# Wide-head attention with three-pass products over two tiles, and its first tiles prepared inside the feed-forward layer before it

## Chip, cores and metric

One core of one Trainium2 chip. The metric is the device time of one execution in microseconds, as a median of several.

## The reference, cut to what matters

Eight layers run one after another on `x` of 32 x 64 tokens of 128 values. With `LN` the plain layer norm, the two that matter are:

```python
# layer 1: feed-forward, 128 -> 512 -> 128
x = x + gelu(LN(x) @ w1 + b1) @ w2 + b2
# layer 2: attention with 16 heads of 64 over the 64 context tokens of the same batch
xn = layernorm(LN(x), ln_gamma, ln_beta)
q = (xn @ w_q).reshape(B, SQ, 16, 64)
k, v = split(ctx @ w_kv)
attn = softmax(einsum('bqhd,bkhd->bhqk', q * 64 ** -0.5, k))
out = einsum('bhqk,bkhd->bqhd', attn, v).reshape(B, SQ, 1024) @ w_out + b_out
x = x + out * tanh(gate)
```

Ahead stands an attention with 16 heads of 8, behind a mixture of 16 experts; four more layers follow. Everything is float32.

## The kernel before

The 2048 tokens are 16 tiles of 128 rows (`NT`), two batches a tile. The residual `X` stays in SBUF. Each engine has its own instruction stream; semaphores order them, and the order within an engine is written out by hand.

`wide_head_attention` is a pipeline over tiles. In step n TensorE does in this order: scores of tile n-2, turned rows of n-1, turned probabilities of n-3, queries of n-1, turned outputs of n-4, keys of n, weighed values of n-3, projection of n-4, values of n-2. Steps 0 to 6 and the last are written out, the rest is a loop of two steps (`pipeline`, `Fori`). Queries (L976) and keys (L939) of a tile are eight float32 products each, of a 128x128 block of weights with 128 columns of tokens; the trace records each float32 product as two instructions. They go through the two PSUM banks `J0` and `J1`, which turned rows (`J0`) and values use too. ScalarE evicts them: L1075 turned rows, L1083 turned probabilities, L1091 queries, L1107 keys, L1099 turned outputs, L1112 exponentials. VectorE has the norms (L139 to L154), the maximum and subtraction (L1157, L1159), the sum, the division, the residual and the copy of the values (L1197). GpSimd computes the reciprocal roots (L150) and copies a tile of context for the values (L1124). TensorE starts the layer (`m.begin`) when the feed-forward layer's last residual addition is done.

`experts` is also the first feed-forward layer (tag `F0`). It already uses three passes instead of a float32 product: operands are split into a high part in the type `fp32r` and a low part (the value less its high part), and L1431 to L1433 add high x high, high x low and low x high in one PSUM group, 512 columns each. The second product (L1464) is float32. Beside it (`beside`) the routing of a later layer is worked out: VectorE's chain `choose` (L1818 to L1846), TensorE's rank products (L1865 to L1867), tables (L1930) fed by GpSimd's `owners` (L1922).

Of the kernel before, what the change touches and what calls it, by code (L numbers as in the profile page):

```python
# [863 lines left out]
def wide_head_attention(sh, m, tag, start, w):  # L864

# [7 lines left out]
    L = Layer()  # L873
    with ExitStack() as scope:
        def sb(name, shape, dt=F32):
            return scope.enter_context(nc.sbuf_tensor(f"{tag}_{name}", shape, dt))

        outer = Norm(sh, sb, f"{tag}_outer", m)
# [4 lines left out]
        qT = sb("qT", [P, 2, HP, P])  # L883
        ctx1 = sb("ctx1", [P, 2, P])
        kT = sb("kT", [P, 2, HP, 2, S])
        v = sb("v", [P, 2, 2, HP, dh])
        prob = sb("prob", [P, 2, H, S])
# [6 lines left out]
        tmp = sb("tmp", [P, 2, P])  # L894

# [14 lines left out]
    x1_ready, xn_ready, xnT_ready, xnT_ps = signal("x1_ready", NT), signal("xn_ready", NT), signal("xnT_ready", NT), signal("xnT_in_psum", NT)  # L910
    q_ps, q_ready = signal("q_in_psum", 2 * NT), signal("q_ready", 2 * NT)
    k_ps, k_ready = signal("k_in_psum", 2 * NT), signal("k_ready", 2 * NT)
    v_ps, v_ready, ctx1_ready = signal("v_in_psum", 2 * NT), signal("v_ready", 2 * NT), signal("ctx1_ready", NT)
# [6 lines left out]
    LO, HI, END = 7, NT - 1, NT + 5  # L920

    def begun(n):

        return isinstance(n, int) and tag in m.stats_after

    def follower():
        return m.stats_after[tag]

    def tensor(pe):
        m.begin(pe, start)  # L930
        pe.wait_ge(*m.dispatch.owner_ready(1))

        def keys(t, p):
# [9 lines left out]
        def values(t, p):  # L943
            pe.wait_ge(*ctx1_ready(t + 1))
            wv = w["v"].rearrange("p (c u d) -> p c u d", u=2, d=dh)
            for b in range(2):
                if before_end(t, 2):
                    pe.wait_ge(*k_ready(2 * t + b + 5))
                elif before_end(t, 1):
                    pe.wait_ge(*q_ready(2 * t + 3 + b))  # L950
                else:
                    pe.wait_ge(*v_ready(2 * t - 1 + b))
                for u in range(2):
                    mm = pe.matmul((J1, J0)[b][u * S:(u + 1) * S, :], ctx1[:, p, b * S:(b + 1) * S], wv[:, :, u, :],  # L954
                                   start=True, stop=True)
                mm.then_inc(v_ps.sem, 1)

        def turn_x(t, p):
            pe.wait_ge(*xn_ready(t + 1))
            if past(t, 2):  # L960
                pe.wait_ge(*v_ready(2 * t - 2))
            else:
                pe.wait_ge(*k_ready(2 * t + 2))
            pe.transpose(J0[:, 0:P], xn[:, p, :], m.ident[:, :]).then_inc(xnT_ps.sem, 1)  # L964

        def queries(t, p):
            pe.wait_ge(*xnT_ready(t + 1))
            for j in range(2):
                if j == 0:
                    if past(t, 2):  # L970
                        pe.wait_ge(*v_ready(2 * t - 3))
                    else:
                        pe.wait_ge(*k_ready(2 * t + 1))
                for c in range(4):
                    cc = 4 * j + c
                    mm = pe.matmul((J1, J0)[j][:, c * P:(c + 1) * P], w["q"][:, cc * P:(cc + 1) * P], xnT[:, p, :],  # L976
                                   start=True, stop=True)
                mm.then_inc(q_ps.sem, 1)

        def scores(t, p):  # L980
            pe.wait_ge(*q_ready(2 * t + 2))
            pe.wait_ge(*k_ready(2 * t + 2))
            if past(t, 1):
                pe.wait_ge(*sub_ready(t))
            apart(pe, m)
            for c in range(HP):
                for b in range(2):
                    for u in range(2):
                        rows, toks = slice(u * S, (u + 1) * S), slice(b * S, (b + 1) * S)
                        mm = pe.matmul(pS[toks, u, c * S:(c + 1) * S], qT[rows, p, c, toks], kT[rows, p, c, b, :],  # L990
                                       start=True, stop=True)
            mm.then_inc(scores_ready.sem, 1)

        def turn_probs(t, p):
            pe.wait_ge(*prob_ready(t + 1))
            if past(t, 2):
                pe.wait_ge(*tmp_ready(t - 1))
            elif past(t, 1):
# [7 lines left out]
        def weigh_values(t, p):  # L1006
            pe.wait_ge(*probT_ready(2 * t + 2))
            pe.wait_ge(*v_ready(2 * t + 2))
            if past(t, 1):
# [10 lines left out]
        def turn_out(t, p):  # L1020
            pe.wait_ge(*on_ready(t + 1))
            if before_end(t, 1):
# [13 lines left out]

        def step(n, p):
            q = 1 - p
            if live(n - 2):
                scores(n - 2, p)  # L1040
            if live(n - 1):
                turn_x(n - 1, q)
            if live(n - 3):
                turn_probs(n - 3, q)
            if begun(n) and n == NT + 2:
                pe.wait_ge(*v_ready(2 * NT))
                follower().turn(pe, 0)
            if live(n - 1):
                queries(n - 1, q)
            if live(n - 4):  # L1050
                turn_out(n - 4, p)
            if live(n):
                keys(n, p)
            if live(n - 3):
                weigh_values(n - 3, q)
            if begun(n) and n == NT + 3:
                follower().turn(pe, 1)
            if live(n - 4):
                project(n - 4, p)
            if live(n - 2):  # L1060
                values(n - 2, p)

        pipeline(pe, step, LO, HI, END)

    def scalar(act):
        m.begin(act, start)

        def step(n, p):
            q = 1 - p
            if live(n - 1):  # L1070
                t = n - 1
                act.wait_ge(*xnT_ps(t + 1))
                if past(t, 2):
                    act.wait_ge(*q_ps(2 * t - 2))
                act.activation(xnT[:, q, :], J0[:, 0:P], ACT.Identity, bias=w["beta"],  # L1075
                               scale=w["gamma"]).then_inc(xnT_ready.sem, 1)
            if live(n - 3):
                t = n - 3
                if past(t, 2):
# [5 lines left out]
            if live(n - 1):  # L1085
                t = n - 1
                if past(t, 2):
                    act.wait_ge(*scores_ready(t - 1))
                for j in range(2):
                    act.wait_ge(*q_ps(2 * t + j + 1))  # L1090
                    act.activation(qT[:, q, 4 * j:4 * j + 4, :].rearrange("p c q -> p (c q)"), (J1, J0)[j],  # L1091
                                   ACT.Copy).then_inc(q_ready.sem, 1)
            if live(n - 4):
                t = n - 4
# [1983 lines left out]
```

## Time and profile before

| | |
|---|---|
| median of 3 runs | 964.1 us (961.65 to 967.59) |
| span of the profiled execution | 1010.8 us, 46.7 above the median |
| TensorE busy | 783.2 us (77%), 8041 instructions |
| VectorE busy | 608.2 us (60%) |
| ScalarE busy | 486.4 us (48%) |
| GpSimd busy | 372.9 us (37%) |
| mean granted TensorE clock | 0.889 of full speed |
| chain that ended last | TensorE 67%, VectorE 9%, ScalarE 5% |

The time of the profiled execution is given as its span alone, from its first to its last instruction. All other times below are from that execution too, in us from its start. A busy share says how long an engine worked, not whether another waited for it.

### The profile page before, as it was taken

To read this page: it belongs to the slowest core of one execution; us is meant where nothing else is said; L and a number is where in the kernel's file an instruction comes from. 1 tells how busy PE (TensorE), PEld (TensorE's weight loads), DVE (VectorE), ACT (ScalarE), POOL (GpSimd) and SP (SyncE) were. 2 spreads that over 40 slices of the span, in tenths; PEclk is the share of its full clock that TensorE was granted. 3 is DMA by queue.
4 is the path that set the end of the run, shared out by engine and by line. 5 is a ranking of instruction groups with operands and counts; after the bars stand their busy time and mean duration, and the time that the engine had idled before them with its cause. 6 is when DMAs were issued, how large, how long until landed. Compare 5 with 4: busy or idle time off the path is not lost.

```text
span 1010.8 us, 24129 instructions
## 1 busy us (share of the span) xinstructions
PE 783.2 (77%) x8041; PEld 646.4 (64%) x8041; DVE 608.2 (60%) x1568; ACT 486.4 (48%) x984; POOL 372.9 (37%) x492
## 2 busy tenths in 40 slices
PE   6998899999999789996477775667677559969005
PEld 3766787888888679985476664667676526644005
DVE  3886747777777667767353224632222368867895
ACT  3886434555444344432154435334444357745753
POOL 5663421111111331111566653155556535550810
PEclk9999699999999979999699989579989769978557
DMA  6300000000000000033332213101111300000001
GB/s 187 96 0 1 1 1 3 2 3 0 0 0 3 1 11 19 21 102 103 95 100 88 64 41 105 42 19 43 40 37 45 85 23 3 0 1 1 0 0 42
DMA packets 49218, 36.06 MB, mean 36 GB/s; under 512 B 7665, under 2 KB 44978, under 8 KB 49138
## 3 DMA queue, kind: packets, MB, share of 16 engines
q1 hardware_dynamic: 43420, 24.45, 8.5%
q0 software_dynamic: 4992, 10.23, 3.6%
q8 instruction: 48, 0.79, 0.3%
q10 hardware_dynamic: 726, 0.33, 0.1%
q14 instruction: 32, 0.26, 0.1%
HBM read 26.73 MB, written 8.26 MB: 35 GB/s over the span
## 4 chain that ended last, share of the span: by engine, by line
PE 67%; DVE 9%; another core or an unknown queue 6%; issue 5%; ACT 5%; DMA 3%; DVEq 2%; POOL 2%; ACTq 1%; SPq 1%; POOLq 0%
PE psum L2118 9%; PE psum L1464 7%; PE psum L2143 4%; PE psum L1034 3%; PE psum L976 3%; PE psum L954 3%; PE psum L939 3%; PE psum L2442 2%; PE psum L1431 2%; PE psum L1432 2%; PE psum L1433 2%; PE psum L323 2%; PE psum L1016 2%; PE psum L663 2%
## 5 line engine op out<-in xcount | busy, mean ns | idle before, releaser
L2118 PE MATMUL psum<-E_XT,E_weights 128*128 128x128 f32 x780 | 114.3, 298 | 52.4 <-ACT E_XT L2198 27.7
L2118 PEld LDWEIGHTS psum<-E_XT,E_weights 128*128 128x128 f32 x780 | 103.0, 209 | 61.2 <-ACT E_XT L2198 30.8
L2266 POOL DMA_INDIRECT y_scratch<-E_y,route_place_of x78 | 78.8, 1010 | 83.2 <-DVE E_y L2321 37.8
L2258 POOL DMA_INDIRECT E_rows<-rows_scratch,route_token_of x78 | 76.4, 979 | 32.1 <-issue 25.5
L1723 DVE SCALAR_TENSOR_TENSOR X<-psum,E_gates,X 128x128 f32<-128x128 f32 x256 | 71.7, 344 | 26.5 <-PE psum L1464 26.4
L1464 PEld LDWEIGHTS psum<-E_w,E_h 128*128 128x128 f32 x512 | 69.4, 198 | 11.5 <-issue 3.5
L2221 ACT ACTIVATE E_h<-psum,cols 128x128 f32<-128x128 f32 x156 | 44.5, 368 | 66.4 <-issue 31.3
L1548 ACT ACTIVATE E_h<-psum,cols 128x512 f32<-128x512 f32 x64 | 43.8, 687 | 67.8 <-PE psum L1433 67.7
L1464 PE MATMUL psum<-E_w,E_h 128*128 128x128 f32 x512 | 70.4, 282 | 4.8 <-DVE X L1723 3.8
L2311 DVE TENSOR_TENSOR E_h<-E_sg,psum 128x384 f32<-128x384 f32 x39 | 21.6, 554 | 77.5 <-remote 26.8
L203 POOL TENSOR_TENSOR rstd<-vareps,nhalf 128x4 f32<-128x4 f32 x24 | 24.6, 1029 | 75.0 <-DVE vareps L197 74.9
L235 PE MATMUL psum<-ident,xn 128*128 128x128 f32 x80 | 20.0, 400 | 35.9 <-ACT xn L226 24.5
L2143 PE MATMUL psum<-L1w,E_h 128*128 x312 | 44.4, 288 | 0.5 <-DVE E_y L2323 0.5
L150 POOL TENSOR_TENSOR A_A_inner_rstd<-A_A_inner_vareps,nhalf 128x1 f32<-128x1 f32 x16 | 8.7, 543 | 95.5 <-DVE A_A_inner_vareps L144 95.5
L788 POOL TENSOR_TENSOR A_kexp<-E_first,hmask 128x512 f32<-128x512 f32 x32 | 32.7, 1042 | 30.0 <-PE psum L663 29.9
L2431 PE MATMUL psum<-ident,Q_amax_rows 128*1 128x128 f32 x5 | 1.7, 332 | 52.1 <-DVE Q_amax_rows L2539 51.4
L235 PEld LDWEIGHTS psum<-ident,xn 128*128 128x128 f32 x80 | 14.0, 210 | 43.5 <-issue 21.5
L2323 DVE TENSOR_TENSOR E_y<-psum,E2b2all 128x128 f32<-128x128 f32 x39 | 11.3, 290 | 49.6 <-PE psum L2143 27.9
L2143 PEld LDWEIGHTS psum<-L1w,E_h 128*128 128x128 f32 x312 | 40.4, 202 | 1.0 <-issue 0.7
L2114 PE MATMUL psum<-ident,E_rows 128*128 128x128 f32 x78 | 22.8, 293 | 22.3 <-DMA E_rows<-rows_scratch,route_token_of 22.3
L2204 ACT ACTIVATE E_weights<-E_first 128x768 f32 x39 | 32.9, 843 | 14.2 <-issue 13.9
L1075 ACT ACTIVATE A_xnT<-psum,cols 128x128 f32<-128x128 f32 x16 | 7.3, 457 | 65.3 <-PE psum L964 65.3
(346 smaller groups left out, 2160.2 us busy)
## 6 DMA issues: line engine op xcount, KB each, us to landing
routed_back<-y_scratch SPq DMA_DIRECT2D x16, 256.0 KB, 4.9
E_first<-in_L_xattn_W SPq DMA_DIRECT2D x1, 2048.0 KB, 8.6
L1w<-in_L_xattn_W SPq DMA_DIRECT2D x8, 256.0 KB, 4.7
rows_scratch<-xn SPq DMA_DIRECT2D x8, 256.0 KB, 2.3
E_w<-in_L_ffn_routed_w SPq DMA_DIRECT2D x28, 64.0 KB, 1.9
E_raw<-in_L_ffn_w_down SPq DMA_DIRECT2D x8, 176.0 KB
E_rows<-rows_scratch,route_token_of POOLq DMA_INDIRECT x78
y_scratch<-E_y,route_place_of POOLq DMA_INDIRECT x78
```

The lines of the kernel that those rows point to most:

```text
L235: tr = pe.transpose(self.bank[:, i * P:(i + 1) * P], self.m.xn[:, g * GT + i, :], self.m.ident[:, :])
L788: ke = pool.tensor_tensor(kexp[:, p, b], kk.broadcast_to([P, HP, S]), m.hmask[:, :].rearrange("p (h o) -> p h o", o=1).broadcast_to([P, HP ...
L939: mm = pe.matmul((J1, J0)[j][:, c * P:(c + 1) * P], w["k"][:, cc * P:(cc + 1) * P], columns(m.ctxT, t, P), start=True, stop=True)
L1464: mm = pe.matmul(y_bank(e, g)[:, i * P:(i + 1) * P], h[:, g % 2, c, i * P:(i + 1) * P], w2[:, p, c, :], start=(c == 0 and i == 0), stop=(c ...
L1548: act.activation(h[:, g % 2, c, :], ring[(C * g + c) % 4], spec["func"], bias=spec["b1"][:, bass.ds(e * C + c, 1)]).then_inc(h_ready.sem, 1)
L1723: st = dve.scalar_tensor_tensor(out=m.X[:, t, :], in0=y_bank(e, g)[:, i * P:(i + 1) * P], scalar=gates[:, t, bass.ds(e, 1)], in1=m.X[:, t, :],
L2118: mm = pe.matmul(out[:, c * P:(c + 1) * P], WE[:, p, (k0 + c) * P:(k0 + c + 1) * P], XT[:, p, :], start=True, stop=True)
L2143: mm = pe.matmul(Y[p][:, 0:P], h[:, p, c, :], W2[:, bass.ds(e, 1), c, :].rearrange("p o d -> p (o d)"), start=c == 0, stop=c == C - 1)
L2204: act.activation(WE[:, i % 2, :], W1[:, bass.ds(e, 1), :].rearrange("p o f -> p (o f)"), ACT.Copy).then_inc(w_ready.sem, 1)
L2221: ac = act.activation(h[:, p, c, :], m.banks[2 + i % 3][:, c * P:(c + 1) * P], spec["func"], bias=spec["b1"][:, bass.ds(e * C + c, 1)])
L2258: pool.indirect_dma_start(out=xg[:, i % 4, :], out_offset=None, in_=rows[:, :], in_offset=bass.IndirectOffsetOnAxis(ap=disp.token_of[:, i: ...
L2266: pool.indirect_dma_start(out=yrows[:, :], in_=y[:, i % 3, :], in_offset=None, out_offset=bass.IndirectOffsetOnAxis(ap=disp.place_of[:, i: ...
```

## The change

In the wide-head attention, queries and keys are made by three `fp32r` passes of 256 columns, over two tiles at once. A step makes half of the head pairs of a pair of tiles: `keys(i)` and `queries(i)` are for pair i // 2 and half i % 2. ScalarE and GpSimd split the context (high parts `CH`, low parts `CL`), the weights (`wide_high`, `wide_low`, in place of the originals) and the rows (`xH`, `xL`). The rows are turned after the probabilities, not ahead of them, and ScalarE evicts them in that order, twice. Keys come ahead of the turned outputs, queries behind them. The values read the context in place, and the copy `ctx1` goes. The pipeline is two steps deeper ahead of the scores and is written out without a loop. The norms of tiles 0 and 1 are computed by VectorE inside the feed-forward layer (`early_rows`), and the keys of four tiles and the queries of two stand ahead of `m.begin` on TensorE. The feed-forward weights get a buffer of their own.

```diff
+        def three(out, wk, cc, xs, start=True):
+            ws = slice(cc * P, (cc + 1) * P)
+            pe.matmul(out, WH[:, wk, ws], xs[0], start=True, stop=False)
+            pe.matmul(out, WH[:, wk, ws], xs[1], start=False, stop=False)
+            return pe.matmul(out, WL[:, wk, ws], xs[0], start=False, stop=True)
+
+        def keys(i, free):
+            pair, half = i // 2, i % 2
+            cols = slice(pair * PW, (pair + 1) * PW)
+            pe.wait_ge(*ctx_low(pair // 2 + 1))
             for j in range(2):
-                if past(t, 1):
-                    pe.wait_ge(*q_ready(2 * t - 1 + j))
-                for c in range(4):
-                    cc = 4 * j + c
-                    mm = pe.matmul((J1, J0)[j][:, c * P:(c + 1) * P], w["k"][:, cc * P:(cc + 1) * P],
-                                   columns(m.ctxT, t, P), start=True, stop=True)
+                if free[j]:
+                    pe.wait_ge(*free[j])
+                for c in range(2):
+                    mm = three((J1, J0)[j][:, c * PW:(c + 1) * PW], 1, 4 * half + 2 * j + c, (CH[:, cols], CL[:, cols]))
                 mm.then_inc(k_ps.sem, 1)
...
+        turn_x(0, None)
+        keys(0, (None, xnT_ready(1)))
+        turn_x(1, k_ready(2))
+        keys(1, (k_ready(1), xnT_ready(2)))
+        queries(0, (k_ready(3), k_ready(4)))
+        queries(1, (q_ready(1), q_ready(2)))
+        keys(2, (q_ready(3), q_ready(4)))
+        keys(3, (k_ready(5), k_ready(6)))
+        m.begin(pe, start)
+
         def step(n, p):
             q = 1 - p
-            if live(n - 2):
-                scores(n - 2, p)
-            if live(n - 1):
-                turn_x(n - 1, q)
-            if live(n - 3):
-                turn_probs(n - 3, q)
...
+            if is_tile(n - 4):
+                scores(n - 4)
+            if is_tile(n - 5):
+                turn_probs(n - 5, q)
+            if n >= 3 and is_tile(n - 1):
+                turn_x(n - 1, v_ready(2 * n - 8) if n >= 5 else xnT_ready(3) if n == 4 else k_ready(8))
...
+            if 5 <= n <= NT:
+                keys(n - 1, (v_ready(2 * n - 9), xnT_ready(n)))
+            if is_tile(n - 6):
+                turn_out(n - 6, p)
+            if n == 4:
+                queries(2, (k_ready(7), xnT_ready(4)))
+            elif 5 <= n <= NT:
+                queries(n - 2, (k_ready(2 * n - 1), k_ready(2 * n)))
+            elif n == NT + 1:
+                queries(n - 2, (v_ready(2 * n - 9), v_ready(2 * n - 8)))
+            if is_tile(n - 5):
+                weigh_values(n - 5, q)
...
     def scalar(act):
+        for s, n in first_products_done:
+            act.wait_ge(s, n)
+        for g in range(NG):
+            cols = slice(g * GW, (g + 1) * GW)
+            act.activation(CH[:, cols], m.ctxT[:, cols], ACT.Copy).then_inc(ctx_high.sem, 1)
...
+        def rows_kept(t):
+            act.wait_ge(*xnT_ps(t + 1))
+            if t >= 4:
+                act.wait_ge(*q_ps(4 * (t // 2) - 4))
+            act.activation(xH[:, t // 2 % 2, t % 2 * P:(t % 2 + 1) * P], J0[:, 0:P], ACT.Identity, bias=w["beta"],
+                           scale=w["gamma"])
+            if t >= 2:
+                act.wait_ge(*x_low(t - 1))
+            act.activation(xnT[:, t % 2, :], J0[:, 0:P], ACT.Identity, bias=w["beta"],
+                           scale=w["gamma"]).then_inc(xnT_ready.sem, 1)
...
+            if n >= 3 and is_tile(n - 1):
+                rows_kept(n - 1)
+            if 5 <= n <= NT:
+                keys_kept(n - 1)
...
     def gpsimd(pool):
+        for t in range(2):
+            outer.rstd(pool, t, t, x1_ready)
+            inner.rstd(pool, t, t, xn_ready)
+        for g in range(NG):
+            cols = slice(g * GW, (g + 1) * GW)
+            pool.wait_ge(*ctx_high(g + 1))
+            pool.tensor_tensor(CL[:, cols], m.ctxT[:, cols], CH[:, cols], ALU.subtract).then_inc(ctx_low.sem, 1)
+
+        def low_part(t):
+            at = slice(t % 2 * P, (t % 2 + 1) * P)
+            pool.wait_ge(*xnT_ready(t + 1))
+            pool.tensor_tensor(xL[:, t // 2 % 2, at], xnT[:, t % 2, :], xH[:, t // 2 % 2, at],
+                               ALU.subtract).then_inc(x_low.sem, 1)
+
+        low_part(0)
+        low_part(1)
         m.begin(pool, start)
...
+    def early_rows(dve, t):
+        outer.stats(dve, tile_of(m.X, t), t, t)
+        outer.apply(dve, x1[:, t, :], tile_of(m.X, t), t, t).then_inc(x1_ready.sem, 1)
+        dve.wait_ge(*x1_ready(t + 1))
+        inner.stats(dve, x1[:, t, :], t, t)
+        inner.apply(dve, xn[:, t, :], x1[:, t, :], t, t).then_inc(xn_ready.sem, 1)
...
@@ experts, gpsimd
         if beside:
+            spec["pool_between"](pool)
             for j in range(NCH):
                 beside.owners(pool, j)
@@ experts, vector, second(e, p, g)
+                if beside and g >= 2:
+                    dve.wait_ge(*combined(1))
+                    m.early_rows(dve, g - 2)
                 dve.wait_ge(*y_ps(u + 1))
@@ build
+        def low_parts(pool):
+            for i, k in enumerate((1, 0)):
+                pool.wait_ge(wide_high_ready, i + 1)
+                pool.tensor_tensor(m.wide_low[:, k, :], wide[:, k, :], m.wide_high[:, k, :], ALU.subtract
+                                   ).then_inc(wide_low_ready, 1)
...
             act.activation(cols[:, 0:row[0]], m.banks[2][:, 0:row[0]], ACT.Copy).then_inc(turned, 1)
+            for k in (1, 0):
+                act.activation(m.wide_high[:, k, :], wide[:, k, :], ACT.Copy).then_inc(wide_high_ready, 1)
             for L in layers[1:]:
                 L.scalar(act)
```

## Rows read from the trace of the kernel before

**Rows 1.** Busy time by stage: feed-forward layer, head of the attention; engines, granted clock, DMA.
```profile
core 0: us, PE busy (x) PEld busy (x) DVE busy (x) ACT busy (x) POOL busy (x), PEclk, DMA share, GB/s
115.40:147.60 32.20, 32.18 (x216) 29.33 (x214) 19.75 (x40) 14.61 (x22) 6.52 (x6) 0.92 0.00 1
147.60:175.00 27.40, 23.38 (x395) 19.30 (x395) 19.04 (x53) 12.68 (x21) 5.60 (x12) 1.00 0.01 2
```
**Rows 2.** Order of time, one attention step: start, length, engine, line, operation.
```profile
244.32 1.16 PE L990 MATMUL psum<-A_kT,A_qT 64*64 64x64 f32 x64
...
245.58 1.04 PE L1001 MATMUL psum<-ident,A_prob 128*128 128x128 f32 x8
245.86 0.46 ACT L1075 ACTIVATE A_xnT<-psum,cols 128x128 f32<-128x128 f32 x1 [4.83 <-PE psum L964]
...
246.22 1.08 ACT L1083 ACTIVATE A_probT<-psum 128x512 f32<-128x512 f32 x2
...
246.45 2.04 PE L976 MATMUL psum<-A_xnT,L1w 128*128 128x128 f32 x16
...
248.33 1.04 PE L1027 MATMUL psum<-ident,A_on 128*128 128x128 f32 x8
...
249.20 1.95 PE L939 MATMUL psum<-ctxT,L1w 128*128 x16
...
250.30 0.60 ACT L1107 ACTIVATE A_kT<-psum 128x512 f32<-128x512 f32 x1 [0.19 <-PE psum L939]
...
251.08 1.16 PE L1016 MATMUL psum<-A_v,A_probT 64*64 64x64 f32 x64
...
254.16 1.94 PE L954 MATMUL psum<-L1w,A_ctx 128*64 128x512 f32 x8
...
256.02 1.16 PE L990 MATMUL psum<-A_kT,A_qT 64*64 64x64 f32 x64
```
**Rows 3.** Order of time on TensorE, three-pass products of the feed-forward layer.
```profile
121.50 0.39 PE L1432 MATMUL psum<-F_XL,F_WH 128*128 128x512 f32 x1
...
122.88 0.39 PE L1432 MATMUL psum<-F_XL,F_WH 128*128 128x512 f32 x1
```
**Rows 4.** Order of time, GpSimd and VectorE in the expert layer.
```profile
354.03 2.67 POOL L1371 TENSOR_TENSOR X<-X,xn 128x512 f32<-128x512 f32 x2
...
354.86 0.71 DVE L1638 TENSOR_TENSOR E_work<-E_logits,E_row 128x224 f32<-128x224 f32 x1
...
355.61 1.35 DVE L1640 TENSOR_TENSOR E_work<-E_work,rev 128x224 f32<-128x224 f32 x1
```
**Rows 5.** Order of time, routing chain in the feed-forward layer.
```profile
117.00 1.27 POOL L249 TENSOR_TENSOR F_XL<-XNT,F_XH 128x512 fp32r<-128x512 f32 x1 [1.08 <-ACT XNT L243]
...
118.78 0.29 DVE L1819 TENSOR_TENSOR route_work<-route_at,route_best 128x128 f32<-128x128 f32 x1
...
119.10 0.29 DVE L1821 TENSOR_TENSOR route_work<-route_work,rev 128x128 f32<-128x128 f32 x1
...
120.96 0.29 DVE L1844 TENSOR_TENSOR route_ahead<-route_upto,route_both 128x128 f32<-128x128 f32 x1
...
123.34 0.38 PE L1865 MATMUL psum<-route_both,earlier 128*128 128x128 f32 x2
```
**Rows 6.** Order of time on TensorE: feed-forward end, first scores, fourth scores.
```profile
143.77 3.82 PE L1464 MATMUL psum<-E_first,F_h 128*128 128x128 f32 x32
...
156.88 1.16 PE L990 MATMUL psum<-A_kT,A_qT 64*64 64x64 f32 x64
...
185.97 1.16 PE L990 MATMUL psum<-A_kT,A_qT 64*64 64x64 f32 x64
```
**Rows 7.** Order of time: fourteenth scores, sixteenth scores, the eviction behind them.
```profile
302.85 1.16 PE L990 MATMUL psum<-A_kT,A_qT 64*64 64x64 f32 x64
...
324.29 1.16 PE L990 MATMUL psum<-A_kT,A_qT 64*64 64x64 f32 x64
...
326.13 1.08 ACT L1083 ACTIVATE A_probT<-psum 128x512 f32<-128x512 f32 x2 [5.03 <-PE psum L1001]
```
**Rows 8.** Groups by line: weight loads of the keys (busy us, mean ns).
```profile
L939 PEld LDWEIGHTS psum<-ctxT,L1w 128*128 128x128 f32 x256 | 29.8, 192 | 1.0 <-DVE X L1719 1.0
```

More of the change, by code:

```diff
@@ L919, in wide_head_attention, with steps, is_tile, turn_x @@
     L.done = x_done(NT)
[L920 to L927, printed above, removed]
+    END = NT + 7
+    first_products_done = m.split_free
+    after = m.stats_after.get
+    def steps(step):
+        for n in range(2, END):
+            step(n, n % 2)
+    def is_tile(t):
+        return 0 <= t < NT
     def tensor(pe):
-        m.begin(pe, start)
         pe.wait_ge(*m.dispatch.owner_ready(1))
-        def keys(t, p):
-            for j in range(2):
-                if past(t, 1):
-                    pe.wait_ge(*q_ready(2 * t - 1 + j))
-                for c in range(4):
-                    cc = 4 * j + c
-                    mm = pe.matmul((J1, J0)[j][:, c * P:(c + 1) * P], w["k"][:, cc * P:(cc + 1) * P],
-                                   columns(m.ctxT, t, P), start=True, stop=True)
-                mm.then_inc(k_ps.sem, 1)
-        def values(t, p):
-            pe.wait_ge(*ctx1_ready(t + 1))
+        pe.wait_ge(*split_weights)
+        def three(out, wk, cc, xs, start=True):
[7 more added lines that the diff above has]
+            pe.wait_ge(*ctx_low(pair // 2 + 1))
+            for j in range(2):
+                if free[j]:
+                    pe.wait_ge(*free[j])
+                for c in range(2):
+                    mm = three((J1, J0)[j][:, c * PW:(c + 1) * PW], 1, 4 * half + 2 * j + c, (CH[:, cols], CL[:, cols]))
+                mm.then_inc(k_ps.sem, 1)
+        def turn_x(t, free):
+            pe.wait_ge(*xn_ready(t + 1))
+            if free:
+                pe.wait_ge(*free)
+            pe.transpose(J0[:, 0:P], xn[:, t % 2, :], m.ident[:, :]).then_inc(xnT_ps.sem, 1)
+        def queries(i, free):
+            pair, half = i // 2, i % 2
+            r = pair % 2
+            pe.wait_ge(*x_low(2 * pair + 2))
+            for j in range(2):
+                pe.wait_ge(*free[j])
+                for c in range(2):
+                    mm = three((J1, J0)[j][:, c * PW:(c + 1) * PW], 0, 4 * half + 2 * j + c, (xH[:, r, :], xL[:, r, :]))
+                mm.then_inc(q_ps.sem, 1)
+        def values(t, n):
@@ L966, in queries @@
[L966 to L978, printed above, removed]
@@ L1058, in step @@
[L1058 to L1063, printed above, removed]
-    def scalar(act):
+            if is_tile(n - 4):
[4 more added lines that the diff above has]
+                turn_x(n - 1, v_ready(2 * n - 8) if n >= 5 else xnT_ready(3) if n == 4 else k_ready(8))
+            if after(tag) and n == NT + 4:
+                pe.wait_ge(*v_ready(2 * NT))
+                after(tag).turn(pe, 0)
@@ L1069, in step @@
             q = 1 - p
[L1070 to L1079, printed above, removed]
+            if is_tile(n - 5):
+                t = n - 5
+                if t >= 2:
                     act.wait_ge(*o_ps(t - 1))
@@ L1100, in step @@
                                    ACT.Copy).then_inc(oT_ready.sem, 1)
[L1101 to L1110 removed]
+            if n >= 4 and is_tile(n - 2):
+                queries_kept(n - 2)
@@ L1130, in step @@
                 outer.rstd(pool, n + 1, 1 - p, x1_ready)
-            if live(n - 1):
-                context(n - 1, 1 - p)
-        outer.rstd(pool, 0, 0, x1_ready)
-        pipeline(pool, step, LO, HI, END)
-        if begun(NT):
+        steps(step)
+        if after(tag):
             for g in range(NG - 1):
-                follower().rstd(pool, g)
+                after(tag).rstd(pool, g)
             for g in range(2):
-                follower().low_part(pool, g)
-                follower().residual(pool, g)
+                after(tag).low_part(pool, g)
+                after(tag).residual(pool, g)
```

224 lines of the change are left out of this document (118 added, 106 removed).

## The prediction

> **What bounds the kernel now.** I read the views in this order: busy time by stage, the order of time on TensorE through one step of the wide-head attention, then the places at its two ends. In the first feed-forward layer TensorE is busy 32.18 of 32.20 us while VectorE has 12 us free [rows 1]. In the attention, one step takes 256.02 - 244.32 = 11.70 us, and each TensorE block starts where the one before it ends [rows 2]: scores and one turned tile 1.26, turned probabilities 0.87, queries 1.88, turned outputs 0.87, keys 1.88, weighing and projection 3.08, values 1.86. ScalarE and VectorE wait for TensorE. So TensorE's order is the clock of the stage, and what counts is whether a removed pass leaves a shorter step or a wait in its place. At the head the queue is not full: from the end of the feed-forward layer (143.77 + 3.82 = 147.59) to the first scores it takes 9.3 us, and 29.1 more to the fourth scores [rows 6].
>
> **Price of a pass.** Before, keys of one tile are 8 products, recorded as 16 instructions of 128 columns, 1.88 us, or 0.117 each [rows 2]. After, a step makes half the keys of two tiles: 4 column groups x 3 passes of 256 columns. No 256-column pass of this type is in the trace. The nearest are the 512-column ones: six of them take 122.88 - 121.50 = 1.38 us, 0.230 each [rows 3]. Half of that is 0.115; if the whole excess over 213 ns (512 columns at 2.4 GHz) belonged to each instruction it would be 107 + 17 = 124 ns. I take 0.117, the price of the old instructions, which have the same 256 column-cycles; bounds 0.107 and 0.125. A block of 12 costs 1.40, a half block 0.70. A step thus sheds 2 x 0.48 = 0.96 us of TensorE work.
>
> The Trainium skill ("TensorE: Matmul & The Clock Gate", Back-to-back issue gap) gives N/2.4 + 2.5 ns, an estimate of 109 ns for 256 columns and 1.31 us for a block. For 512 columns it gives 216, and the rows show 230, so I keep the rows.
>
> **Where the shed time goes.** The new step is: scores, turned probabilities, turned rows, keys half a, keys half b, turned outputs, queries, weighing, projection, values. Keys b write the bank in which the turned rows stand, so they wait for `xnT_ready`. ScalarE now evicts the turned probabilities first, then the rows twice (high part, full value). From the start of the scores: where turned probabilities follow the scores directly, the first eviction starts 326.13 - 324.29 = 1.84 us later [rows 7]. Two evictions start 0.49 apart (1.08 for two, 0.60 for one), so the rows start at 1.84 + 0.98 = 2.82; two of them 0.36 apart, the last 0.46 long [rows 2], end at 3.64, and TensorE is released at 3.69. It gets there at 1.09 + 0.87 + 0.16 + 0.70 = 2.82. That is a new stall of 0.87 us. Restarting costs an estimated 0.13. The step is 3.69 + 0.13 + 0.70 + 0.87 + 1.40 + 3.08 + 1.86 = **11.73 us**, against 11.70. Nearly all that the passes save is spent on the wait. Queued behind it are all later TensorE blocks of the step, and ScalarE and VectorE wait for those. The weighing starts 6.79 after the scores, where it was 6.76, so VectorE's chain is as before. GpSimd's new low part of the rows (a quarter of 1.27 [rows 5], 0.32; with its start 0.5 at most) is there before the queries, which start 1.57 after keys b. The copy `ctx1` on GpSimd goes, at no gain: nothing waits long for it.
>
> **First feed-forward layer.** GpSimd gets two subtractions of 128x1024 behind its last low part. One of 128x512 takes 1.27 [rows 5], so 2.53 each. At that point VectorE is in the routing chain that TensorE needs. The rows show what happens then: while GpSimd subtracts or adds two SBUF tensors, a VectorE operation with two SBUF inputs does not finish. During two such GpSimd operations (354.03, 2.67 for both), a VectorE one from 354.86 takes 0.71, and the next, from 355.61, takes 1.35 and ends when GpSimd does [rows 4]. Each long operation catches one short one. Here the first subtraction runs from about 118.4 to 120.9 and catches L1819 (118.78, alone 0.29); the second runs to 123.5 or so and catches L1821, which ends at 123.9 and not 119.39. The rest of the chain to the end of L1844 (121.25) took 1.86 after L1821, so it ends at 125.8. TensorE wants it at 123.34 [rows 5] and is full there [rows 1]: **+2.5 us**. If the order fell luckily it would be 0; if the later chain (bias addition, slots, tables) also came too late, up to 4.2.
>
> The Trainium skill ("SBUF — State Buffer", Who interferes with whom) says the same of a `tensor_tensor` with two SBUF inputs against GpSimd's reads: an exclusive lock for the whole instruction. It speaks against these two subtractions. Without it the 2.5 would be 0; rows 4 agree with it.
>
> Costed at nothing there: the early norms of two tiles, in VectorE's free 12 us (if they were late, the residual additions behind them would be, and nothing on TensorE waits for those); two ScalarE copies of 128x1024 before TensorE has anything turned; another buffer for the weights; the four ScalarE copies of the context, behind its last activation.
>
> **Head of the attention.** Counted from the end of TensorE's feed-forward work. GpSimd finishes the norm of tile 1 about then, and the first of four context low parts is there 0.5 later. Turned tile 0, keys 0, turned tile 1, keys 1 alternate with evictions, to about 5. Queries 0 wait for two low parts of rows behind 4 x 1.27 of context on GpSimd: 5.2. From there eight half blocks run on two banks, each bank needing 0.70 + 0.16 + 0.60 + 0.18 before reuse (0.16: first half of the keys done at 250.14, eviction at 250.30 [rows 2]), so 0.82 each, 6.6; the last eviction and one turned tile: 1.0. First scores at 12.8, against 9.3: **+3.5**. The wait for TensorE's begin of the layer costs nothing more.
>
> From the first scores to the second: 1.25 to the turned rows, 1.2 for their eviction, 0.5 for GpSimd's low part, queries half a 0.7 and its eviction 0.9, values 1.9: 6.5. To the third: 1.09 + 0.87 + 0.16 + 0.70, wait to 3.8, 0.70, queries 1.6, weighing 1.1, values 1.9: 9.2. To the fourth 11.7. Together 27.4, against 29.1 [rows 6]: **-1.7**. The routing indices, which VectorE did inside this stretch, now fall into the head.
>
> **Middle and tail.** Ten steps from the fourth scores (185.97) to the fourteenth (302.85) took 116.9 [rows 6, 7]; now 117.3: **+0.4**. To the sixteenth it took 21.4 [rows 7]. Now the step of the fourteenth scores has queries but no keys, with the turned outputs held by the eviction before them: 10.3. The next has neither: 9.0, the same as the last before. Together 19.3: **-2.1**. What follows has the same order as before.
>
> **Sum.** 2.5 + 3.5 - 1.7 + 0.4 - 2.1 = +2.6 us. The profiled span is 1010.8, so 1013.4 after; the median of three runs is 964.1, 46.7 less. I carry the difference over one to one, as it arises where TensorE and not a transfer sets the pace: 966.7. A change of this kernel can be told from none at about 1%, 9.6 us.
>
> **Rivals.**
> - *The stall doesn't arise.* If the rows are evicted by the time of keys b, each of eleven steps is 0.87 shorter (ScalarE's evictions would have to overlap more than rows 2 show): -9.6, so 957.1. For it: ScalarE is not full. Against: its order is fixed and every gap above is a measured one. 0.13.
> - *GpSimd's subtractions catch nothing that TensorE needs.* -2.5: 964.2. 0.10.
> - *Weight loads show (the other side).* A load is recorded at 0.192 [rows 8]. If a 256-column pass of this type cost that instead of 0.117, a half block is 0.45 longer: 3 x 0.45 x 11 = 14.9 in full steps, 3 in the steps around them and 4.4 in the head, 22.4 in all: 989. Each 10 ns costs 3 us, so it passes +1% from 0.140 a pass. Against: the old 128-column instructions have the same recorded load and run at 0.117. 0.08.
> - *The clock falls in the head.* With gaps between half blocks and a 2.5 us pause before, TensorE could be granted 1.2 GHz; twelve half blocks then cost about 0.6 more each, +7: 974. Against: 23.38 busy of 27.40 in the old head kept 1.00 [rows 1]. 0.07.
>
> **How the numbers follow.** The forecast case has 0.62, with its own range 962 to 971 (pass 0.107 to 0.125: -3.0 to +2.4; layer stall 0 to 4.2; head +-2). The range 956 to 974 takes in the missing stall and the clock case and leaves out the dear passes and what lies beyond on the low side. Faster by over 1% needs both of the first two rivals or cheaper passes besides: 0.07. Slower by over 1%: the dear passes, half of the clock case, a little of the forecast: 0.13. Within 1%: 0.80.
>
> **What would show it.** Right: TensorE idle about 0.9 us ahead of the second half of the keys in each step, released by ScalarE's `xnT`; steps of 11.6 to 11.8; a pause near 2.5 us before L1865; passes 0.117 apart; the first scores near 166 us. Wrong: steps near 10.8 (no stall), passes over 0.14, a granted clock under 1 in the head, or an early end of the feed-forward layer.

## The result, and the profile after

The changed kernel takes 968.9 us (median of 14 runs, 966.9 to 974.8); the kernel before takes 961.7 (14 runs, 959.7 to 967.6, on the same chip). The ratio is 1.0070, interval 1.0054 to 1.0086: 6.7 us slower. The forecast was 966.7, inside one per cent of before, with +2.6 us as the sum of its terms. The median of before is 2.4 us lower in these 14 runs than in the three that the forecast started from, so the forecast time is closer than the forecast difference: the sum is short by some 4 us.

The profiled execution spans 969.1 us. That of before (1010.8) has some 48 us more in the later stage of dispatched experts, which the change doesn't touch and which is left aside here. Up to the last scores of the attention the two traces can be laid side by side.

First the busy times of the changed kernel, then busy time by window (feed-forward layer, head, and two stretches of the head), to be read against [rows 1]:

```profile
PE 772.1 (80%) x7913; PEld 627.5 (65%) x7913; DVE 613.2 (63%) x1568; ACT 495.7 (51%) x1006; POOL 386.1 (40%) x498
```
```profile
core 0: us, PE busy (x) PEld busy (x) DVE busy (x) ACT busy (x) POOL busy (x), PEclk, DMA share, GB/s
116.20:149.40 33.20, 31.76 (x214) 28.66 (x212) 26.32 (x55) 15.90 (x26) 14.31 (x12) 0.93 0.00 1
149.40:176.80 27.40, 22.16 (x246) 17.56 (x246) 14.91 (x45) 14.92 (x29) 10.19 (x17) 0.88 0.01 1
162.00:168.00 6.00, 3.09 (x73) 2.80 (x73) 3.98 (x10) 1.61 (x4) 1.92 (x4) 0.75 0.01 3
168.00:180.00 12.00, 11.38 (x177) 7.95 (x178) 7.38 (x18) 6.95 (x12) 2.09 (x4) 0.84 0.01 2
```

The feed-forward layer now has a gap on TensorE. The head, where the clock was full before, has a stretch at 0.75: between 162 and 180 us TensorE works for a part of the time at 1.2 GHz.

Next the order of time on TensorE in the changed kernel (start, length, engine, line, operation): the end of the feed-forward layer and the first, second, third, fourth, fourteenth and sixteenth scores, to be read against [rows 6, 7].

```profile
145.57 3.82 PE L1530 MATMUL psum<-F_weights,F_h 128*128 128x128 f32 x32
...
161.98 1.16 PE L994 MATMUL psum<-XNT,xn 64*64 64x64 f32 x64
...
172.36 1.16 PE L994 MATMUL psum<-XNT,xn 64*64 64x64 f32 x64
...
181.50 1.16 PE L994 MATMUL psum<-A_kT,A_qT 64*64 64x64 f32 x64
...
193.26 1.16 PE L994 MATMUL psum<-A_kT,A_qT 64*64 64x64 f32 x64
...
311.39 1.16 PE L994 MATMUL psum<-XNT,xn 64*64 64x64 f32 x64
...
330.85 1.16 PE L994 MATMUL psum<-A_kT,A_qT 64*64 64x64 f32 x64
```

Differences of these starts give each stretch its length (the sum is worked out unrounded, 330.85 - 324.29):

| stretch | before | after | difference | forecast |
|---|---|---|---|---|
| to the end of the feed-forward layer | 147.59 | 149.39 | +1.8 | +2.5 |
| from there to the first scores | 9.3 | 12.6 | +3.3 | +3.5 |
| first to fourth scores | 29.1 | 31.3 | +2.2 | -1.7 |
| fourth to fourteenth | 116.9 | 118.1 | +1.2 | +0.4 |
| fourteenth to sixteenth | 21.4 | 19.5 | -2.0 | -2.1 |
| sum | | | +6.6 | +2.6 |

The sum of the trace agrees with the 6.7 us of the ratio. That it agrees to a tenth is luck: what follows the last scores takes between 634 and 640 us in the profiled runs of the changed kernel and of the experiments below. One term has the wrong sign: first to fourth scores. Its three steps are 10.38, 9.14 and 11.76 where the forecast had 6.5, 9.2 and 11.7, so all of it lies in the first of them. The order of time there, ScalarE, GpSimd, VectorE and TensorE of the changed kernel:

```profile
163.06 0.45 POOL L1176 TENSOR_TENSOR A_xnT_split<-A_xnT,A_xnT_split 128x128 fp32r<-128x128 f32 x1 [3.05 <-ACT A_xnT L1108]
...
163.47 0.54 POOL L150 TENSOR_TENSOR A_A_outer_rstd<-A_A_outer_vareps,nhalf 128x1 f32<-128x1 f32 x1
163.83 0.45 ACT L1108 ACTIVATE A_xnT<-psum,cols 128x128 f32<-128x128 f32 x1
164.05 0.35 DVE L154 TENSOR_SCALAR A_x<-X,A_A_outer_meanvar,A_A_outer_rstd 128x128 f32<-128x128 f32 x1 [1.73 <-POOL A_A_outer_rstd L150]
...
165.33 0.54 POOL L150 TENSOR_TENSOR A_A_inner_rstd<-A_A_inner_vareps,nhalf 128x1 f32<-128x1 f32 x1 [1.31 <-DVE A_A_inner_vareps L144]
165.84 0.46 POOL L1176 TENSOR_TENSOR A_xnT_split<-A_xnT,A_xnT_split 128x128 fp32r<-128x128 f32 x1
166.34 0.58 PE L940 MATMUL psum<-A_xnT_split,L1w_high 128*128 128x256 f32 x1 [2.91 <-POOL A_xnT_split L1176]
...
166.72 0.42 PE L941 MATMUL psum<-A_xnT_split,L1w_high 128*128 128x256 f32 x1
166.94 0.42 PE L942 MATMUL psum<-A_xnT_split,L1w_low 128*128 128x256 f32 x1
...
169.21 3.22 PE L979 MATMUL psum<-L1w,ctxT 128*64 128x512 f32 x8
```

The row of tile 3 is there at 164.28 (the L1108 from 163.83). GpSimd could make its low part at once, but its order puts `inner.rstd` of tile 4 first. That waits for VectorE's statistics of tile 4, these wait for `outer.rstd` of tile 4 (163.47), and that stood behind the low part of tile 2. So the low part comes at 165.84, and TensorE, which wants it for queries of tiles 2 and 3, stands for 2.91 us. Behind the pause its passes start 0.21 apart instead of 0.117: the granted clock has fallen.

And the steady step (TensorE and ScalarE), to be read against [rows 2]:

```profile
240.51 1.16 PE L994 MATMUL psum<-A_kT,A_qT 64*64 64x64 f32 x64
...
242.36 1.09 ACT L1139 ACTIVATE A_probT<-psum 128x512 f32<-128x512 f32 x2 [5.14 <-PE psum L1005]
...
242.56 0.37 PE L940 MATMUL psum<-E_XH,L1w_high 128*128 128x256 f32 x1
242.77 0.28 PE L941 MATMUL psum<-E_XL,L1w_high 128*128 128x256 f32 x1
242.89 0.28 PE L942 MATMUL psum<-E_XH,L1w_low 128*128 128x256 f32 x1
...
243.24 0.28 PE L942 MATMUL psum<-E_XH,L1w_low 128*128 128x256 f32 x1
243.33 0.46 ACT L1104 ACTIVATE A_xnT_split<-psum,cols 128x128 fp32r<-128x128 f32 x1
...
243.67 0.47 ACT L1108 ACTIVATE A_xnT<-psum,cols 128x128 f32<-128x128 f32 x1
...
244.20 0.39 PE L940 MATMUL psum<-E_XH,L1w_high 128*128 128x256 f32 x1 [0.68 <-ACT A_xnT L1108]
244.42 0.28 PE L941 MATMUL psum<-E_XL,L1w_high 128*128 128x256 f32 x1
...
245.80 0.36 PE L940 MATMUL psum<-A_xnT_split,L1w_high 128*128 128x256 f32 x1
...
247.39 1.16 PE L1020 MATMUL psum<-A_v,A_probT 64*64 64x64 f32 x64
```

TensorE has finished the first half of the keys and stands still until ScalarE's second copy of the rows is out, 3.69 us after the scores (244.20 - 240.51), which is the figure of the forecast. The groups of instructions between 180 and 310 us count the same wait over eleven steps:

```profile
L940 PE MATMUL psum<-E_XH,L1w_high 128*128 128x256 f32 x44 | 14.4, 328 | 7.4 <-ACT A_xnT L1108 7.4
```

### The profile page after: what moved, and what is told of

The parts are those of the page before. It is cut to its first block, busy times and chain, and to the rows that moved or that the text cites. A ratio compares the mean times of both kernels' runs of the same rounds, so it can differ in the third digit from the quotient of the medians.

```text
span 969.1 us, 23578 instructions
## 1 busy us (share of the span) xinstructions
PE 772.1 (80%) x7913; PEld 627.5 (65%) x7913; DVE 613.2 (63%) x1568; ACT 495.7 (51%) x1006; POOL 386.1 (40%) x498
## 4 chain that ended last, share of the span: by engine, by line
PE 55%; POOL 14%; issue 9%; DVE 9%; ACT 7%; DMA 4%; SPq 1%; ACTq 1%; DVEq 0%; POOLq 0%
PE psum L1530 7%; POOL y_scratch L2336 6%; POOL E_rows L2328 5%; PE psum L1038 3%; PE psum L979 3%; PE psum L2188 3%; PE psum L2512 2%; PE psum L323 2%; PE psum L1020 2%; PE psum L2213 2%; PE psum L1497 2%; PE psum L1499 2%; ACT A_probT L1139 2%; PE psum L994 2%; PE psum L1498 2%
## 5 line engine op out<-in xcount | busy, mean ns | idle before, releaser
L2188 PE MATMUL psum<-E_XT,E_weights 128*128 128x128 f32 x780 | 103.5, 281 | 1.5 <-DVE E_XT L2366 0.8
L2188 PEld LDWEIGHTS psum<-E_XT,E_weights 128*128 128x128 f32 x780 | 96.3, 197 | 2.9 <-DVE E_XT L2366 1.5
L1139 ACT ACTIVATE A_probT<-psum 128x512 f32<-128x512 f32 x32 | 17.4, 596 | 77.2 <-PE psum L1005 77.2
L1645 POOL CAST E_WH<-E_w 128x128 fp32r<-128x128 f32 x16 | 4.7, 291 | 91.7 <-DMA E_w<-in_L_ffn_routed_w 72.3
```

The costliest lines, as they stand in the source:

```text
L1139: act.activation(probT[:, q, 4 * half:4 * half + 4, :].rearrange("p c q -> p (c q)"), pP[:, half, :], ACT.Copy).then_inc(probT_ready.sem, 1)
L2188: mm = pe.matmul(out[:, c * P:(c + 1) * P], WE[:, p, (k0 + c) * P:(k0 + c + 1) * P], XT[:, p, :], start=True, stop=True)
```

## Experiments

Every kernel was compared with the kernel before on the same chip. A per cent is 9.6 us. The kernels ran in three groups (the changed kernel by itself; then `rows_first`, `low_first`, `weights_early` and `all_three`; then the rest), each with its own runs of the kernel before, whose medians are 961.7, 964.0 and 962.6 us. So kernels are compared by their ratios and not by their times. `all_three` has 5 runs, `weights_rows` 6 and each other one 12 or 14. Two theories stood at the start: the steady step is held by ScalarE's order ahead of the second half of the keys (against: TensorE or VectorE would hold it anyway), and the second scores are late by GpSimd's order (against: by the clock or by VectorE alone).

| kernel | ratio to before | interval |
|---|---|---|
| changed kernel | 1.0070 | 1.0054 to 1.0086 |
| `rows_first` | 0.9939 | 0.9915 to 0.9963 |
| `low_first` | 1.0064 | 1.0038 to 1.0090 |
| `weights_early` | 1.0019 | 1.0001 to 1.0036 |
| `weights_low` (last two together) | 0.9991 | 0.9972 to 1.0010 |
| `weights_rows` | 0.9906 | 0.9870 to 0.9941 |
| `all_three` | 0.9873 | 0.9847 to 0.9900 |
| `two_pass` | 0.9970 | 0.9941 to 0.9999 |
| `before_unrolled` | 0.9970 | 0.9951 to 0.9989 |

**1. The rows ahead of the probabilities** (`rows_first`). TensorE turns the rows first, and ScalarE evicts them first.

```diff
 # TensorE, step(n)
-            if is_tile(n - 5):
-                turn_probs(n - 5, q)
             if n >= 3 and is_tile(n - 1):
                 turn_x(n - 1, ...)
+            if is_tile(n - 5):
+                turn_probs(n - 5, q)
 # ScalarE, step(n)
+            if n >= 3 and is_tile(n - 1):
+                rows_kept(n - 1)
             if is_tile(n - 5):
...
-            if n >= 3 and is_tile(n - 1):
-                rows_kept(n - 1)
```

> The changed kernel with one thing put back: TensorE turns the rows ahead of the probabilities, and ScalarE evicts the rows ahead of them. Theory A (the wait of the second half of the keys for the turned rows eats what the passes save): no wait is left there, a full step goes from 11.82 to about 10.9 us, 11 steps give 10 us, so 958 to 960, under the kernel before. Rival B (VectorE, busy 9.0 us of a step, is next): steps of 11.3 or more, 963 to 965. Rival C (the stall is no cost, the same time is lost behind it): 968 to 969.

Measured: 959.0 us, ratio 0.9939, 1.3% under the changed kernel. Order of time of one step of `rows_first`:

```profile
234.85 1.16 PE L994 MATMUL psum<-A_kT,A_qT 64*64 64x64 f32 x64
...
236.67 0.45 ACT L1108 ACTIVATE A_xnT<-psum,cols 128x128 f32<-128x128 f32 x1
...
237.57 0.28 PE L942 MATMUL psum<-E_XH,L1w_low 128*128 128x256 f32 x1
237.69 0.28 PE L940 MATMUL psum<-E_XH,L1w_high 128*128 128x256 f32 x1
237.81 0.28 PE L941 MATMUL psum<-E_XL,L1w_high 128*128 128x256 f32 x1
...
245.72 1.16 PE L994 MATMUL psum<-XNT,xn 64*64 64x64 f32 x64
```

The rows are out at 237.12, before TensorE has even ended the first half of the keys; the second half follows 0.12 later with no wait, and the step is 245.72 - 234.85 = 10.87. It was 11.82: 0.95 is gone from each step. The recorded idle time was 0.68, but counted from start to start the stall was 0.84 (244.20 - 243.24 - 0.117). The last 0.1 is the restart: behind the wait the second pass starts 0.22 after the first (244.42 - 244.20), here 0.12 after it (237.81 - 237.69). Over the steps from the second scores on this is 11 us; the ratio gives 12.6, with some 3 us of uncertainty. The first theory holds: the stall is why fewer passes brought nothing.

**2. GpSimd's order at tiles 2 to 4** (`low_first`).

```diff
+            if n == 4:
+                low_part(n - 1)
             if is_tile(n):
                 inner.rstd(pool, n, p, xn_ready)
-            if n >= 3 and is_tile(n - 1):
+            if n == 3:
+                outer.rstd(pool, n + 1, 1 - p, x1_ready)
+            if n >= 3 and n != 4 and is_tile(n - 1):
                 low_part(n - 1)
-            if is_tile(n + 1):
+            if n != 3 and is_tile(n + 1):
                 outer.rstd(pool, n + 1, 1 - p, x1_ready)
```

> The changed kernel, with GpSimd's order changed in the two steps around the first scores alone: the outer root of tile 4 ahead of the low part of tile 2, the low part of tile 3 ahead of the inner root of tile 4. Theory A (TensorE's 2.9 us pause ahead of queries 2 is GpSimd's queue order, and the clock falls to 1.2 GHz after it): queries 2 start about 1.3 us earlier, the clock stays at 2.4 GHz, first to second scores 6.5 to 7.5 us instead of 10.4, so 965 to 966. Rival B (the clock falls anyway, as the head's pauses sum up): 1.3 us less alone, 967.6. Rival C (no gain, another wait comes up): 969.

Measured: 969.0 us, ratio 1.0064: no gain to speak of (0.6 us by the two ratios, uncertain by some 3). Yet in its trace the second scores follow the first after 6.42 us (165.50 to 171.92), at a granted clock of 1.00, near the 6.5 that the forecast had for the changed kernel. Most of the 4.0 us gained there was lost earlier in this profiled execution, in the feed-forward layer. The rank products on TensorE in `low_first`, then in the changed kernel:

```profile
125.50 0.80 PE L1939 MATMUL psum<-route_both,earlier 128*128 128x128 f32 x2 [2.73 <-DVE route_ahead L1918]
```
```profile
124.95 0.49 PE L1935 MATMUL psum<-route_both,earlier 128*128 128x128 f32 x2 [1.44 <-DVE route_ahead L1914]
```

and the windows behind this pause in `low_first`:

```profile
124.00:130.00 6.00, 4.50 (x21) 4.50 (x22) 5.60 (x14) 0.00 (x0) 0.00 (x0) 0.59 0.00 0
130.00:136.00 6.00, 6.00 (x34) 5.49 (x34) 4.56 (x10) 2.08 (x4) 0.59 (x1) 0.84 0.00 0
```

Here the clock is low around the end of the pause and behind it (0.59, then 0.84); the feed-forward layer ended 3.0 us later, counted from its first product. The edit itself lies behind this place in GpSimd's order and can't have caused it. Whether the other eleven executions lost time at the same place isn't known. So this run leaves the size of the second theory open, and the pause had to go first.

**3. The weights split ahead of the feed-forward layer** (`weights_early`). GpSimd makes the high parts too.

```diff
         def low_parts(pool):
             for i, k in enumerate((1, 0)):
+                pool.tensor_copy(m.wide_high[:, k, :], wide[:, k, :]).then_inc(wide_high_ready, 1)
                 pool.wait_ge(wide_high_ready, i + 1)
...
-            spec["pool_between"](pool)
...
             pool.wait_ge(loaded, NLOAD)
+            low_parts(pool)
...
-            for k in (1, 0):
-                act.activation(m.wide_high[:, k, :], wide[:, k, :], ACT.Copy).then_inc(wide_high_ready, 1)
```

> The changed kernel with the split of the query and key weights (high copies and subtractions) moved to GpSimd ahead of the feed-forward layer, where it is idle, so that no long GpSimd subtraction stands beside VectorE's routing chain. Theory A (two VectorE operations are held by them): L1889 and L1891 take 0.29 again, TensorE's pause of 1.4 us ahead of the rank products goes, 967.3. Rival B (the GpSimd work ahead of the layer delays the norms or the attention's tail): 969 to 971.

Measured: 964.8 us, ratio 1.0019, 0.5% (5 us) under the changed kernel, more than was expected. The routing chain on VectorE, first in the changed kernel with GpSimd's two subtractions, then in `weights_early`, to be read against [rows 5]:

```profile
118.05 4.85 POOL L2934 TENSOR_TENSOR L1w_low<-L1w,L1w_high 128x1024 fp32r<-128x1024 f32 x2
...
118.59 2.04 DVE L1889 TENSOR_TENSOR route_work<-route_at,route_best 128x128 f32<-128x128 f32 x1
120.67 2.38 DVE L1891 TENSOR_TENSOR route_work<-route_work,rev 128x128 f32<-128x128 f32 x1
```
```profile
117.56 0.29 DVE L1888 TENSOR_TENSOR route_work<-route_at,route_best 128x128 f32<-128x128 f32 x1
117.88 0.29 DVE L1890 TENSOR_TENSOR route_work<-route_work,rev 128x128 f32<-128x128 f32 x1
...
119.75 0.29 DVE L1913 TENSOR_TENSOR route_ahead<-route_upto,route_both 128x128 f32<-128x128 f32 x1
...
121.60 0.38 PE L1934 MATMUL psum<-route_both,earlier 128*128 128x128 f32 x2
```

Each subtraction caught one VectorE operation, as the forecast had it, and the chain ended 3.8 us later, counted from the layer's first product. The two calls of 2.37 us now lie between 85 and 91 us, in the layer ahead, where GpSimd is free; TensorE's rank products follow the first products without a pause. The Trainium skill ("SBUF — State Buffer", Who interferes with whom) says that a VectorE instruction with two SBUF inputs contends with a GpSimd instruction that reads SBUF. This trace agrees with it: 2.04 and 2.38 us against 0.29.

Where the 5 us lie can be read from the traces. The last scores come 4.8 us sooner than in the changed kernel (326.09 for 330.85): the feed-forward layer starts 1.0 sooner, takes 2.5 less from its first product to its last (31.6 for 34.1), and the second scores follow the first after 9.15 and not 10.38, because the clock is back sooner (the values take 2.00 us there and 3.22 in the changed kernel). Not all of this is due to the edit. In the four profiled runs without the pause (`weights_early`, `weights_low`, `weights_rows`, `all_three`) the layer takes 31.1 to 32.1 us. In the two of them that keep GpSimd's order the step to the second scores takes 9.15 and 9.37.

**4. GpSimd's order again, without the pause** (`weights_low`: the edits of 2 and 3).

> Weights split ahead of the feed-forward layer and GpSimd's order changed for tiles 2 to 4 (norm before low part, low part before norm), TensorE's order as in the changed kernel. Theory A (the late low part of tile 3 is worth the difference of the second scores, 9.15 to 6.4, and it holds once the pause in the feed-forward layer is gone): 2.7 us under the version with early weights alone, a ratio to the kernel before of 0.999. Rival B (what is gained at the second scores is lost by the fourth, where VectorE or ScalarE is late): same as early weights alone, ratio 1.002.

Measured: ratio 0.9991, 0.28% (2.7 us) under `weights_early`, as the second theory had it. That the tenth is right too is luck, since the intervals overlap and the difference is uncertain by 2 us or more; what the trace shows is the step to the second scores, 9.15 in `weights_early` and 6.41 here. The second scores of `weights_low`, and the wait ahead of queries 2:

```profile
159.74 1.16 PE L994 MATMUL psum<-XNT,xn 64*64 64x64 f32 x64
...
162.62 0.39 PE L940 MATMUL psum<-A_xnT_split,L1w_high 128*128 128x256 f32 x1 [1.43 <-POOL A_xnT_split L1176]
...
166.15 1.16 PE L994 MATMUL psum<-XNT,xn 64*64 64x64 f32 x64
```

6.41 us again. The third and fourth scores follow after 9.15 and 11.75, so nothing is given back. The same edit on top of the other two is worth 0.33% (`all_three` against `weights_rows`, whose intervals overlap as well), and in the traces this step falls from 9.37 to 6.42.

**5. The edits together** (`weights_rows`: 1 and 3; `all_three`: 1, 2 and 3).

> Weights split ahead of the feed-forward layer, and the rows turned and evicted ahead of the probabilities, GpSimd's order in the attention as in the changed kernel. If the two edits are independent their differences add: -9.9 for the rows and -4.1 for the weights, ratio to the kernel before 0.990. Rival (part of the weights' gain is a clock fall that the other edit also cures): ratio 0.993. Against the version with all three edits (0.987) the GpSimd order would be worth 3 us by the first, 5 or more by the second.

> The three edits together. Theory A: their gains add, 10 + 3.5 + 1.6, so about 954. If they share a cause, 957 to 959.

Measured: 0.9906 and 0.9873, so the two bigger edits add within the uncertainty. `all_three` takes 951.9 us, 1.3% (12 us) less than the kernel before and 2% less than the changed kernel: the work is the change's own, only the order is different. Its steps are 10.87 us against 11.70 of before. A part of the 1.3% isn't due to the products: the kernel before with its loop written out (experiment 7) has a ratio of 0.9970, and against that `all_three` is 1.0% shorter.

**6. One product left out** (`two_pass`). Queries and keys are less exact by it; the kernel serves to price a pass.

```diff
             pe.matmul(out, WH[:, wk, ws], xs[0], start=True, stop=False)
-            pe.matmul(out, WH[:, wk, ws], xs[1], start=False, stop=False)
             return pe.matmul(out, WL[:, wk, ws], xs[0], start=False, stop=True)
```

> Leaves out one of the three products of keys and queries (high part of the weights by low part of the operand), so queries and keys are less exact. A step loses 8 passes of 256 columns; 2 of them lie in the first half of the keys, ahead of the wait for ScalarE's second copy of the rows, where they are hidden by it. Theory A (TensorE's own work sets the step outside the stall): the step is 11.82 - 6 x 0.117 = 11.1 us, the stall before the keys' second half grows from 0.68 to 0.9, and the eleven steps and the head bring the time about 9 us under the changed kernel, near 960. Rival B (no cover, every pass counts): 11.82 - 0.94 = 10.9, near 957. Rival C (the step is held by ScalarE and VectorE and TensorE only waits elsewhere): the step stays above 11.5 and the time above 966.

Measured: 960.6 us, ratio 0.9970, 1.0% under the changed kernel. The step is 11.10 and the wait as expected, 0.91:

```profile
245.46 1.16 PE L993 MATMUL psum<-XNT,xn 64*64 64x64 f32 x64
...
249.14 0.39 PE L940 MATMUL psum<-E_XH,L1w_high 128*128 128x256 f32 x1 [0.91 <-ACT A_xnT L1107]
```

So a pass outside the stall is worth its 0.117 us in full, and one ahead of the stall (2 of the 8) nothing: the start after the wait is still 3.68 us behind the scores (249.14 - 245.46).

**7. The loop of before written out** (`before_unrolled`): its fixed steps are issued one by one, with the same work in the same order.

```diff
-    LO, HI, END = 7, NT - 1, NT + 5
+    LO, HI, END = NT - 1, NT - 1, NT + 5
...
-        pipeline(pe, step, LO, HI, END)
+        pipeline_out(pe, step, LO, HI, END)    # for n in range(0, END): step(n, n % 2)
```

> The kernel before with the hardware loop of the wide-head attention written out, its products and their order kept. Theory A (the loop costs next to nothing): steps of 11.6 to 11.7 us and a time within 2 us of the kernel before. Rival (a jump back costs each engine a fetch, so that the loop's removal was worth a gain that hid a larger loss of the products): steps 0.3 or more shorter, 3 us or more in all.

Measured: ratio 0.9970 (-2.9 us, between -4.7 and -1.1). Its steps are 11.61 throughout; in before the first two behind the fourth scores are 11.62 and 11.61 and those of the loop 11.70. The last scores come 0.96 earlier. The first theory holds for the steps; the time is 2.9 us shorter where it allowed 2, with an interval that takes in both. Where the rest of the 2.9 us lies, if it is more than chance, isn't found. The changed kernel has no loop either. Against 11.61 its step of 11.82 is 0.2 longer, so the end of the loop hides a part of what the new step loses.

## Why the prediction held, and where not

- **Price of a pass: right.** 0.117 us in the steady step (242.77, 242.89 and so on to 243.24), as taken. The estimate of 109 ns for these from the Trainium skill ("TensorE: Matmul & The Clock Gate", Back-to-back issue gap) is not what the rows show; the page gives its formula for a single product by itself. The rival of dear weight loads falls: the loads of these passes are recorded at 0.19 and the passes still start 0.117 apart.
- **The new stall: right, and shown.** Forecast: release 3.69 us behind the scores, stall 0.87. Measured: 3.69; 0.84 from start to start. Experiment 1 took it away and with it 0.95 per step, restart included (0.1; the forecast had 0.13 for it). The rival "the stall doesn't arise" (957) falls, but its time is close to that of `rows_first`: what it got wrong was only that ScalarE's order would allow it.
- **Middle: size off by 0.8.** The step is 11.82 for 11.73 (+0.9 in ten steps). The twelve passes of the queries take 247.39 - 245.80 = 1.59 and not 1.40: 0.2 more at the change from and to other products. The turned outputs take 0.79, not 0.87. Ten steps make +1.2 for +0.4.
- **Feed-forward layer: right in mechanism, size near.** Both operations were caught, the chain ended at 124.90 for a forecast of 125.8; +1.8 for +2.5 in the profiled run. But the edit that removes it was worth 5 us, and 0.7% where the GpSimd order was mended as well. The price of the pause isn't one number (experiment 3 and the last section).
- **Head: right.** 12.6 for 12.8 (forecast +3.5, measured +3.3), and by the forecast's parts: the queries start 4.8 us after the end of the layer for 5.2, and the eight half blocks of queries and keys follow 0.84 apart for 0.82. No experiment was made for the head.
- **First to second scores: the step that failed.** "Queries half a 0.7 and its eviction 0.9, values 1.9: 6.5" counted 0.5 us for GpSimd's low part, as if GpSimd were free. The operation itself takes 0.46; but it stood behind the inner root of tile 4, and this behind VectorE's statistics and the outer root of the same tile, a chain that the forecast hadn't followed: 10.38 measured. Of the 3.9 us, 1.5 are the longer pause (2.91 against 1.43 in `weights_low`). Twelve passes at 0.213 for 0.117 make 1.2, and eight value products at half clock 1.3 more (3.22 us by the trace, for 1.94): together 2.5 for the clock. The rival "the clock falls in the head" (974, 0.07) named the effect and the place nearly; it expected the fall ahead of the first scores and for another reason. Experiments 2 and 4 show the cause: the order alone brings 6.4 and the full clock.
- **Tail: right.** 19.5 for 19.3.
- **The whole:** +2.6 forecast, +6.6 in the trace, +6.7 by the ratio. The missed wait and the clock behind it alone make 3.9; the other terms are off by +0.8, -0.7, -0.2 and +0.1 and cancel. That the forecast time (966.7) is only 2.2 under the measured one owes as much to luck: it started from a median of before that was 2.4 too high. The rival "GpSimd's subtractions catch nothing" (964) falls with experiment 3.

## What to carry to other kernels

Where a product is split into cheaper passes, follow the second operand to its maker. The saved time can come back as a wait at the first bank or buffer that the shorter block now reaches too soon. Here the order of two evictions decided whether 0.95 us per step were won or lost. On an engine with little to do (GpSimd here at 40%) look at what stands ahead in its queue, not at its load: a waiting norm held back a 0.46 us operation for 1.6 us (164.28 to 165.84). And ask of every idle stretch on TensorE what clock it gets behind it.

## What the runs showed of the hardware

The clock and a pause. In the head, a pause of 2.9 us on TensorE came with a fall in the profiled runs of the changed kernel, `rows_first`, `weights_early` and `weights_rows` (0.71 to 0.75 granted between 162 and 168 us) and of `two_pass` (0.81), and a pause of 1.43 with none in `weights_low` and `all_three` (1.00). In the changed kernel the granted clock falls while TensorE still stands; two windows inside the pause (163.43 to 166.34; the granted clock is 1.00 in the first and 0.50 in the second):

```profile
163.50:165.00 1.50, 0.00 (x0) 0.00 (x0) 0.77 (x3) 0.78 (x2) 0.51 (x2) 1.00 0.04 11
165.10:166.30 1.20, 0.00 (x0) 0.00 (x0) 1.20 (x2) 0.00 (x0) 0.96 (x2) 0.50 0.00 0
```

In `weights_rows` the first passes behind the pause still start 0.22 and 0.16 apart, and the later ones 0.21, so there the clock falls just behind its end.

In the feed-forward layer the changed kernel's pause of 1.44 and that of 1.65 in `rows_first` cost no clock. One of 2.73 in `low_first` did, and one of 2.72 in `two_pass` did not (1.00 from 124 to 130 us). So at 2.7 us the length of the pause alone doesn't tell. How often the clock falls in the runs that weren't profiled isn't known. The times don't tell either: they spread from 965 to 978 in `low_first`, and as widely in `two_pass` (953 to 966).

A pause grows when TensorE is quick. In the feed-forward layer TensorE reaches 2.4 GHz at 120.6 us in the changed kernel and at 118.3 in `low_first`: the step between its passes changes from 0.43 to 0.23 us there. Counted from the layer's first product (115.27 and 115.83), that is after 5.4 and 2.5 us. VectorE's chain ends 9.6 us after that product in both, but TensorE's last pass ahead of the wait starts after 7.9 us in the one and 6.6 in the other, so the quicker TensorE waits longer, 2.73 us for 1.44. In `two_pass` the full clock comes after 2.1 us and the pause is 2.72. This is read from the traces; no run was made for it alone.
